# Landmark softmax in groups of two batches, two projection banks, zero matmuls in TensorE's waits, and half of the first attn1 exponentials inside the loop

## The chip, the cores and the metric

The kernel runs on one NeuronCore of a Trainium2 chip, as one program. The metric is the device time of one execution in microseconds (us); the time of a kernel is the median of its timed runs. Engines: PE is TensorE (PEld its weight load), DVE VectorE, ACT ScalarE, POOL GpSimd, SP SyncE. PS is PSUM, eight banks of 512 fp32 columns in 128 partitions.

## What is computed

Eight batches of small images and texts go through a tokenizer, a Nystrom attention layer (8 heads of 32), a mixture of experts, a second attention layer and a second mixture. The change touches the Nystrom attention. Cut to what matters:

```python
q_l = q.reshape(b, HEADS, LANDMARKS, l, DIM_HEAD).mean(3)
k_l = k.reshape(b, HEADS, LANDMARKS, l, DIM_HEAD).mean(3)
attn1 = softmax(einsum('bhid,bhjd->bhij', q, k_l), -1)
attn2 = softmax(einsum('bhid,bhjd->bhij', q_l, k_l), -1)
attn3 = softmax(einsum('bhid,bhjd->bhij', q_l, k), -1)
# _pinv(attn2): z0 scaled by the max of row and column sums over ALL batches and heads, then 6 steps:
az = a @ z
z = 0.25 * z @ (13.0 * I - az @ (15.0 * I - az @ (7.0 * I - az)))
out = attn1 @ attn2_inv @ (attn3 @ v) + conv(v)
```

The scale of the pseudo-inverse is a maximum over all batches. So attn2 of all eight batches must be ready before the first iteration of the first batch.

## The kernel before, in words

The block has a prologue and a loop over the eight batches (`body(b)`). Each engine has its own list of instructions, written out by hand in the order in which it runs them; semaphores (`wait_ge`, `then_inc`) tie the lists together. An engine that waits holds up everything behind it in its list.

Prologue, attn2. `proj(p, part)` (L740) projects the landmark tokens of a pair p of batches, part 0 for q and part 1 for k, into bank 4. ScalarE copies it out (`copied`, L919 and L921), and the next projection waits for that copy, since there is one bank. `scores(i)` (L752) makes the 8 heads' scores of batch i in banks 0 to 3. DVE takes the maximum (`shifted`, L1136) and subtracts it for half of the heads (L1141). ScalarE takes the exponential of four heads straight from PSUM, one instruction a head with its own bias and sum (`halved`, L930), and of the other four in one instruction (L934). `scores(i+1)` waits for both readers (`n_sub`, `n_half`). DVE sums and inverts (`summed`, L1149 to L1161), POOL multiplies (`normalised`, L985, signals `n_a`), TensorE adds row sums up (`sums`, L761). After the eighth batch DVE takes the maximum, TensorE spreads it (L791), DVE makes the scale `RCK` (signals `n_rck`), and ScalarE applies it in `opened` (L878).

Along with this the prologue does the front of batch 0: `project` (L561), `values` (L569), `scores3` (L583), `top3` (L1029) and `exps3` (L812) for attn3; `scores1` (L594), `top1` (L1040), `exps1` (L826) for attn1; `turn3` transposes (L601), `turned3`, `weigh` (L611), `turn_weighed` (L619), `small` (L1076), and `start` (L659).

Loop. A pass has 12 steps of TensorE (L677), k = 0 to 11, two per iteration of the inverse, each in two halves of four heads. An even step is read by DVE into NN (L1106); an odd one is added to TD and becomes ST (L1112). TD comes from POOL (L977), which needs SA, a scaling of ST on ScalarE (L895) that stands at the head of each iteration. Between the steps the table `FRONT` places the front of batch b+1, and `BACK` the end of batch b-1. In pass 0 alone `ffn_bias` (L636) and `value_out` (L644), both for later stages, and `turn1(0)` (L629) stand between the steps too. `start(b+1)` ends the pass.

Of the kernel before, what the change touches and what calls it, by code (L numbers as in the profile page):

```python
# [110 lines left out]
def program(nc, xpatch, txt, w1, ln1, vec, mat, wide, const, taps, out):  # L111
    with ExitStack() as ctx:
# [29 lines left out]
        WU = sb("WU", [1, 3])  # L142

# [18 lines left out]
        AA = fs("AA", [128, B, H, SW])  # L162

# [57 lines left out]
        with nc.Block() as block:  # L221
# [307 lines left out]
        SCORES, PROJ, PINV, TAIL = 0, 4, 4, 6  # L529
        SUMS, TOPS = 3, 1  # L530
# [17 lines left out]

        def quad(b, rows, width):

            return PS[0:rows, bank(b, 0):bank(b, 0) + 4, 0:width]

        with nc.Block() as block:
            @block.tensor
            def _(pe):

                def project(b):
                    if b:
                        pe.wait_ge(sem("f_pt"), upto(b - 1, 2, 2))
                    for j in range(4):  # L560
# [6 lines left out]
                def values(b):  # L567
                    for t in range(2):
                        last = nc.tensor.matmul(PS[0:UT, bank(b, 3), t * 256:(t + 1) * 256],  # L569
                                                XAP[:, b // 2, t * UT:(t + 1) * UT],  # L570
                                                MA[:, qkv(b) + 512:qkv(b) + 768], start=True, stop=True)
                    last.then_inc(sem("f_v"), 1)

                def scores3(b):
                    pe.wait_ge(sem("f_q"), upto(b, 1, 1))
# [22 lines left out]
                def turn3(b, t):  # L598
                    pe.wait_ge(sem("f_e1"), upto(b, 2, t + 1))
# [104 lines left out]
                def out_proj(b):  # L704

                    pe.wait_ge(sem("f_oo"), upto(b, 1, 1))
                    for hh in range(2):
# [5 lines left out]
                         9: weigh, 10: turn_weighed}  # L713
                BACK = {3: lambda b: attend(b, 0), 4: lambda b: attend(b, 1), 6: out_proj}

                def body(b):
                    for k in range(STEPS):
                        step(b, k // 2, k % 2)
                        if b == 0 and k == 0:
                            pe.wait_ge(sem("n_rck"), 1)  # L720
# [7 lines left out]
                        if b + 1 < B and k in FRONT:  # L728
                            FRONT[k](b + 1)
# [4 lines left out]
                def proj(p, part):  # L734
                    if 2 * p + part:
                        pe.wait_ge(sem("n_qk"), 2 * p + part)
                    for j in range(2):
                        for o in range(2):
                            w = qkv(o) + (2 * part + j) * 128
                            last = nc.tensor.matmul(PS[:, PROJ, (2 * j + o) * KP:(2 * j + o + 1) * KP], MA[:, w:w + 128],  # L740
# [3 lines left out]
                def scores(i):  # L744
                    pe.wait_ge(sem("n_qk"), 2 * (i // 2) + 2)
                    if i:
                        pe.wait_ge(sem("n_sub"), i)
                        pe.wait_ge(sem("n_half"), i)
                    for h in range(H):
                        r, hh = h % 4, h // 4  # L750
                        rows = slice(32 * r, 32 * r + 32)
                        last = nc.tensor.matmul(PS[0:KP, SCORES + r, hh * KP:(hh + 1) * KP], QL[rows, i // 2 % 3, hh, i % 2, :],  # L752
                                                QL[rows, i // 2 % 3, 2 + hh, i % 2, :], start=True, stop=True)
# [1519 lines left out]
```

## Time and profile before

| | us |
|---|---|
| median of 3 runs (728.40 to 735.58) | 730.26 |
| profiled execution | 736.04 |
| its span | 734.2 |
| PE busy | 681.5 (93%) |
| DVE, ACT, POOL busy | 413.5, 377.6, 229.7 |
| mean granted clock of TensorE | 0.939 |

Read it so: the profiled execution is some 6 us above the median of the runs, and sums are made against it. TensorE is busy for 93% of the span, but the share is a mean over stages. The page's row of the granted clock, in 40 slices of 18.4 us, shows where the clock was lower: `PEclk9997699999999999999958999957999999996999`. The fourth and fifth slices (55 to 92 us) are this block's prologue.

### The profile page before, as it was taken

How to read it: one execution, taken by the hardware profiler on the slowest of the kernel's cores; microseconds unless marked ns; L12 is line 12 of the kernel's file. 1: busy time of each engine (PE TensorE's matmuls, PEld its weight loads, DVE VectorE, ACT ScalarE, POOL GpSimd, SP SyncE). 2: the span in 40 equal slices, each digit the busy share in tenths (PEclk: the TensorE clock that was granted, in tenths of full speed). 3: DMA queues.
4: the chain of work that ended last, by engine and by line, in shares of the span. 5: the costliest groups of instructions: out<-in, count | busy, mean ns of one | idle time of the engine just before them, and what ended most of it. 6: DMA issues, size and time to landing. Idle time of an engine off the chain costs nothing. (4 is left out here: it accounts for less than half of the span.)

```text
span 734.2 us, 15178 instructions
## 1 busy us (share of the span) xinstructions
PE 681.5 (93%) x6033; PEld 527.5 (72%) x6033; DVE 413.5 (56%) x843; ACT 377.6 (51%) x1035; POOL 229.7 (31%) x204
## 2 busy tenths in 40 slices
PE   9887898999999999999889999869999999989896
PEld 5676798988989898988785555557666666647555
DVE  3457347667575767674525333426777777764322
ACT  4656447565655647473246555335555455544531
POOL 4155325343544344444300434023222222201001
PEclk9997699999999999999958999957999999996999
DMA  8200000000000000000000000000000000000000
GB/s 267 99 3 1 1 1 3 2 1 2 1 2 2 2 1 3 2 1 2 1 1 1 1 1 1 1 1 1 1 1 1 1 2 1 1 1 1 1 15 17
DMA packets 5214, 8.23 MB, mean 11 GB/s; under 512 B 3608, under 2 KB 4120, under 8 KB 4760
## 3 DMA queue, kind: packets, MB, share of 16 engines
q1 hardware_dynamic: 4552, 7.20, 3.1%
q8 instruction: 48, 0.79, 0.4%
q14 instruction: 22, 0.18, 0.1%
q10 hardware_dynamic: 592, 0.07, 0.1%
HBM read 6.71 MB, written 0.55 MB: 10 GB/s over the span
## 5 line engine op out<-in xcount | busy, mean ns | idle before, releaser
L977 POOL TENSOR_TENSOR STD<-STD,NN 91x492 f32<-91x492 f32 (+1 forms) x96 | 104.0, 1101 | 149.2 <-DVE NN L1106 78.7
L677 PE MATMUL PS<-ST 128*91 128x123 f32 x768 | 92.9, 272 | 4.8 <-DVE ST L1112 4.6
L1106 DVE SCALAR_TENSOR_TENSOR NN<-ST,PS 91x492 f32<-91x492 f32 x96 | 62.9, 661 | 56.3 <-PE PS L677 56.3
L677 PE MATMUL PS<-NN 128*91 128x123 f32 (+1 forms) x768 | 89.6, 268 | 3.2 <-DVE NN L1106 3.2
L677 PEld LDWEIGHTS PS<-ST 128*91 128x91 f32 x768 | 83.5, 159 | 11.0 <-DVE ST L1112 7.1
L677 PEld LDWEIGHTS PS<-NN 128*91 128x91 f32 x768 | 82.2, 160 | 10.4 <-DVE NN L1106 6.4
L1746 PE MATMUL PS<-QR,KA 128*128 128x270 f32 x256 | 72.2, 413 | 0.0
L895 ACT ACTIVATE STD<-ST 91x492 f32<-91x492 f32 (+1 forms) x96 | 51.6, 569 | 39.6 <-DVE ST L1112 39.6
L1860 DVE TENSOR_SCALAR CL<-PS,K 128x270 f32<-128x270 f32 x144 | 65.7, 496 | 9.8 <-PE PS L1746 4.5
L1112 DVE SCALAR_TENSOR_TENSOR ST<-PS,STD 91x492 f32<-91x492 f32 (+1 forms) x96 | 55.9, 599 | 22.1 <-POOL STD L977 12.4
L1801 ACT ACTIVATE EX<-CL,NG 128x540 f32<-128x540 f32 x64 | 46.7, 741 | 32.8 <-DVE CL L1860 32.7
L1508 ACT ACTIVATE GE<-PS,FB 128x540 f32<-128x540 f32 x64 | 42.4, 707 | 35.1 <-PE PS L1413 34.9
L1677 POOL TENSOR_TENSOR QR<-QR 64x540 f32<-64x540 f32 x32 | 34.6, 1082 | 68.4 <-ACT QR L1792 68.4
L1746 PEld LDWEIGHTS PS<-QR,KA 128*128 128x128 f32 x256 | 46.2, 194 | 10.8 <-issue 2.9
L826 ACT ACTIVATE E_<-PS,M 71x91 f32<-71x91 f32 x128 | 40.4, 344 | 9.8 <-DVE M L1040 9.8
L1413 PE MATMUL PS<-XM,MF 64*128 64x270 f32 x256 | 40.7, 440 | 0.1
L1837 DVE COPY KA<-PS 64x288 f32<-64x288 f32 x64 | 29.1, 454 | 20.3 <-PE PS L1687 17.9
L812 ACT ACTIVATE E<-PS,M 91x142 f32<-91x142 f32 x64 | 23.0, 372 | 28.5 <-DVE M L1029 28.5
L1761 PE MATMUL PS<-EX,VM 128*64 128x270 f32 x256 | 36.2, 404 | 0.0
L1433 PE MATMUL PS<-GE,WI 128*64 128x270 f32 x256 | 35.8, 403 | 0.0
L1413 PEld LDWEIGHTS PS<-XM,MF 64*128 64x128 f32 x256 | 23.1, 197 | 15.8 <-issue 8.2
L1792 ACT ACTIVATE QR<-PS 64x270 f32<-64x270 f32 x64 | 24.8, 388 | 18.5 <-PE PS L1687 18.1
(326 smaller groups left out, 1250.5 us busy)
## 6 DMA issues: line engine op xcount, KB each, us to landing
TP<-taps SPq DMA_DIRECT2D x1, 1204.0 KB, 16.1
MA<-mat SPq DMA_DIRECT2D x1, 1120.0 KB, 7.5
MF<-mat SPq DMA_DIRECT2D x1, 1024.0 KB, 12.6
WI<-wide SPq DMA_DIRECT2D x1, 902.0 KB, 9.0
CO<-const SPq DMA_DIRECT2D x1, 512.0 KB, 15.7
MQ<-mat SPq DMA_DIRECT2D x1, 512.0 KB, 16.4
out<-OS SPq DMA_DIRECT2D x8, 45.0 KB
XA<-xpatch SPq DMA_DIRECT2D x1, 256.0 KB, 2.8
```

The costliest lines, as they stand in the source:

```text
L677: last = nc.tensor.matmul(PS[0:NL, PINV + q, h % 4 * SW + c0:(h % 4 + 1) * SW], x[:, h, 0:NL], x[:, h, c0:SW], start=True, stop=True)
L826: last = nc.scalar.activation(E1_[:, h, t, :], PS[0:UT, bank(b, r), c:c + NL], ACT.Exp, bias=M1[:, hh, r, t:t + 1], accum_out=Z1[:, 0, 2 * ...
L895: nc.scalar.mul(SA[:, 4 * q:4 * q + 4, c0:SW], ST[0:NL, b % 2, 4 * q:4 * q + 4, c0:SW], S_D).then_inc(sem("f_sa"), 1)
L977: nc.gpsimd.tensor_tensor(TD[:, 4 * q:4 * q + 4, c0:SW], SA[:, 4 * q:4 * q + 4, c0:SW], NN[0:NL, 4 * q:4 * q + 4, c0:SW], ALU.subtract).th ...
L1106: v.scalar_tensor_tensor(out=NN[0:NL, own, :], in0=ST[0:NL, b % 2, own, :], scalar=N_S, in1=heads4(PS[0:NL, PINV + q, 0:4 * SW]), op0=ALU. ...
L1112: v.scalar_tensor_tensor(out=ST[0:NL, b % 2, own, c0:SW], in0=heads4(PS[0:NL, PINV + q, 0:4 * SW])[:, :, c0:SW], scalar=S_M, in1=TD[:, own ...
L1413: last = nc.tensor.matmul(PS[:, HIDDEN + 2 * (j % 2) + o, 0:NP], MF[half, j * 128:(j + 1) * 128], XM[half, p, :], start=True, stop=True)
L1508: nc.scalar.activation(GE[:, ring(p, j), :, :], PS[:, HIDDEN + 2 * (j % 2):HIDDEN + 2 * (j % 2) + 2, 0:NP], ACT.Gelu, bias=FB1[:, j:j + 1] ...
L1746: last = nc.tensor.matmul(PS[:, bank, 0:NP], KA[:, a, u, t * 128:(t + 1) * 128], QR[:, a, u, :], start=True, stop=True)
L1761: last = nc.tensor.matmul(PS[t * D:(t + 1) * D, 7 * o, 0:NP], VM[:, o, t, u * D:(u + 1) * D] if u < H else VR[:, o, t, :], EX[:, slot(i, o ...
L1801: nc.scalar.activation(EX[:, n, :, :], CL[:, n, :, :], ACT.Exp, scale=NG[:, u:u + 1]).then_inc(sem("d_e"), 1)
L1860: v.tensor_scalar(CL[:, slot(i, o, u), t, :], PS[:, bank, 0:NP], K2[:, a, c:c + 1], 0.0, ALU.add, ALU.max).then_inc(sem("d_cl"), 1)
```

## The change

Four edits, all in the prologue and the first pass.

1. The softmax of attn2 goes by pairs. `scores(p)` makes 16 matmuls, for both batches, in the same four banks (4 x 96 columns of each); `shifted`, `halved`, `other_half` and `summed` work on both, so each runs four times on twice the elements. `normalised` still works on one batch, two in a row.
2. `PROJ` becomes two banks, 4 for part 0 and 7 for part 1; a projection waits for the copy of its own bank. `values(0)` writes bank 5, and `scores1(0)` banks 0 to 3. The orders of TensorE, ScalarE and DVE in the prologue are written out anew; `small(0)` and `start(0)` move ahead of the scale. POOL does its five memsets at the start.
3. `spin(n, bank, low)`: n matmuls of zeros (256 columns, fp32, 32 output partitions that nothing reads), 1, 2, 2, 3 and 2 of them at five places of TensorE's list.
4. `exps1(0, 0)` stays in the prologue, behind `weighed(0)`; `exps1(0, 1)`, `total1`, `inverse1` and `normal1` of batch 0 go into iteration 0 of pass 0, and `turn1(0)` from step 0 to step 3. For this pass a table `FIRST` takes the place of `FRONT`, with the front of batch 1 one step later. Banks 1 to 3 still hold attn1's scores of batch 0, so `project(1)` waits for both halves of `exps1(0)`.

```diff
-        SCORES, PROJ, PINV, TAIL = 0, 4, 4, 6
-        SUMS, TOPS = 3, 1
+        SCORES, PROJ, PINV, TAIL = 0, (4, 7), 4, 6
+        SUMS, TOPS = 3, 4
...
                 def project(b):
-                    if b:
+                    if b > 1:
                         pe.wait_ge(sem("f_pt"), upto(b - 1, 2, 2))
+                    elif b:
+                        pe.wait_ge(sem("f_e1"), 2)
...
+                FIRST = {1: lambda b: (project(b), values(b)), 3: scores3, 6: scores1, 8: lambda b: turn3(b, 0), 9: lambda b: turn3(b, 1),
+                         10: weigh, 11: turn_weighed}
...
-                def scores(i):
-                    pe.wait_ge(sem("n_qk"), 2 * (i // 2) + 2)
-                    if i:
-                        pe.wait_ge(sem("n_sub"), i)
-                        pe.wait_ge(sem("n_half"), i)
+                def scores(p):
+                    pe.wait_ge(sem("n_qk"), 2 * p + 2)
+                    if p:
+                        pe.wait_ge(sem("n_sub"), p)
+                        pe.wait_ge(sem("n_half"), p)
...
+                FIRST = {1: query, 3: exps3, 7: lambda b: exps1(b, 0), 8: lambda b: exps1(b, 1), 9: turned3, 10: weighed}
...
-                def halved(i):
-
-                    act.wait_ge(sem("n_max"), i + 1)
-                    if i >= 2:
-                        act.wait_ge(sem("n_a"), i - 1)
-                    for h in (0, 1, 4, 5):
+                def halved(p):
+
+                    act.wait_ge(sem("n_max"), p + 1)
+                    if p >= 2:
+                        act.wait_ge(sem("n_a"), 2 * p - 2)
+                    for r in range(2):
+                        for g in range(4):
...
                 FRONT = {0: (key,), 1: (value,), 2: (top3,), 4: (total3,), 5: (top1, inverse3), 8: (total1, inverse1),
                          10: (small,)}
+                FIRST = {1: (key, value), 3: (top3,), 5: (total3,), 6: (top1, inverse3), 9: (total1, inverse1),
+                         11: (small,)}
```

TensorE's order in the last part of the prologue. Before, from the seventh scores (L752) on; L761 is `sums`, L601 `turn3`, L611 `weigh`, L791 the scale, L619 `turn_weighed`, L659 `start(0)`:

```order
L752 MATMUL PS<-STD 96x96 x8
L761 MATMUL PS<-AA,SL 32x91 x8
L752 MATMUL PS<-STD 96x96 x8
L761 MATMUL PS<-AA,SL 32x91 x8
L601 MATMUL PS<-CO,E 71x91 x16
L761 MATMUL PS<-AA,SL 32x91 x16
L611 MATMUL PS<-P,VU 32x91 x16
L791 MATMUL PS<-CG,ON 91x32
L619 MATMUL PS<-CO,WX 91x128 x2
L659 MATMUL PS<-AA 91x123 x8
```

Now, from the fourth and last scores (L778) on; L787 is `sums`, L169 the zeros, L611 `scores1(0)`, L621 `turn3`, L631 `weigh`, L639 `turn_weighed`, L679 `start(0)`, L828 the scale:

```order
L778 MATMUL PS<-STD 96x96 x16
L787 MATMUL PS<-AA,SL 32x91 x16
L169 MATMUL PS<-ZK 32x256 x3
L611 MATMUL PS<-KM,QM 71x91 x16
L621 MATMUL PS<-CO,E 71x91 x16
L787 MATMUL PS<-AA,SL 32x91 x16
L631 MATMUL PS<-P,VU 32x91 x16
L787 MATMUL PS<-AA,SL 32x91 x8
L639 MATMUL PS<-CO,WX 91x128 x2
L787 MATMUL PS<-AA,SL 32x91 x8
L679 MATMUL PS<-AA 91x123 x8
L828 MATMUL PS<-CG,ON 91x32
```

`scores1(0)` has come behind the last scores of attn2, and `start(0)` ahead of the scale.

TensorE's order in pass 0, steps 2 to 7 (a step is the row of eight matmuls 91x123). Before (L636 `ffn_bias`, L583 `scores3(1)`, L644 `value_out`, L594 `scores1(1)`, L677 a step):

```order
L677 MATMUL PS<-ST 91x123 x8
L636 MATMUL PS<-VE,MF 128x1 x16
L583 MATMUL PS<-KM,QM 91x142 x8
L677 MATMUL PS<-NN 91x123 x8
L644 MATMUL PS<-MV 64x64 x16
L677 MATMUL PS<-ST 91x123 x8
L677 MATMUL PS<-NN 91x123 x8
L594 MATMUL PS<-KM,QM 71x91 x16
L677 MATMUL PS<-ST 91x123 x8
```

Now (L656 `ffn_bias`, L649 `turn1(0)`, L664 `value_out`, L596 `scores3(1)`, L611 `scores1(1)`, L697 a step):

```order
L697 MATMUL PS<-ST 91x123 x8
L656 MATMUL PS<-VE,MF 128x1 x16
L697 MATMUL PS<-NN 91x123 x8
L649 MATMUL PS<-CO,P 91x71 x16
L664 MATMUL PS<-MV 64x64 x16
L596 MATMUL PS<-KM,QM 91x142 x8
L697 MATMUL PS<-ST 91x123 x8
L697 MATMUL PS<-NN 91x123 x8
L697 MATMUL PS<-ST 91x123 x8
L611 MATMUL PS<-KM,QM 71x91 x16
L697 MATMUL PS<-NN 91x123 x8
```

`scores3(1)` has moved from behind step 2 to behind step 3 and what follows it, and `scores1(1)` from behind step 5 to behind step 6.

ScalarE's order in pass 0, now (L933 the scaling into SA at the head of an iteration, two rows of it being the two halves; L848 `exps3(1)`, L863 `exps1(1)`, L905 and L902 parts for later stages):

```order
L848 ACTIVATE E,Z<-PS,M 91x142 x8
L933 ACTIVATE STD<-ST 91x492 x2
L905 ACTIVATE MF<-MF,VE 128x256
L902 ACTIVATE WH<-PS,VE 128x512
L933 ACTIVATE STD<-ST 91x492 x2
L905 ACTIVATE MF<-MF,VE 128x256
L863 ACTIVATE E_,Z<-PS,M 71x91 x8
L933 ACTIVATE STD<-ST 91x492 x2
L905 ACTIVATE MF<-MF,VE 128x256
L863 ACTIVATE E_,Z<-PS,M 71x91 x8
```

Before, both halves of `exps1(1)` stood ahead of the third of these scalings; now one stands on each side of it.

## Rows read from the trace of the kernel before

**Rows 1.** Table of stretches: busy us (instructions) by engine, granted clock, DMA.

```profile
core 0: us, PE busy (x) PEld busy (x) DVE busy (x) ACT busy (x) POOL busy (x), PEclk, DMA share, GB/s
36.40:53.50 17.10, 15.42 (x169) 13.62 (x169) 8.57 (x20) 9.12 (x37) 9.95 (x10) 1.00 0.01 2
...
56.90:67.20 10.30, 10.00 (x111) 9.07 (x110) 7.01 (x18) 7.34 (x41) 5.11 (x4) 0.50 0.01 2
...
74.00:84.50 10.50, 9.04 (x77) 7.81 (x77) 3.91 (x13) 4.03 (x16) 1.40 (x1) 0.50 0.01 2
...
87.70:101.30 13.60, 12.88 (x109) 12.04 (x108) 5.33 (x8) 5.28 (x10) 5.18 (x5) 1.00 0.00 1
101.30:126.70 25.40, 23.07 (x277) 21.08 (x277) 18.51 (x31) 17.82 (x69) 10.73 (x9) 0.93 0.01 2
126.70:160.90 34.20, 33.48 (x406) 30.46 (x404) 23.46 (x41) 20.16 (x72) 15.58 (x13) 1.00 0.01 2
```

**Rows 2.** Timeline, TensorE: start, us, shape, records (two a matmul), idle before.

```profile
36.43 1.10 PE L740 MATMUL PS<-XAP,MA 128*128 128x96 f32 x8 [1.09 <-PEq L127]
...
39.90 0.59 PE L752 MATMUL PS<-STD 32*96 32x96 f32 x16 [0.66 <-ACT STD L919]
...
45.59 1.03 PE L569 MATMUL PS<-MA,XAP 128*71 128x256 f32 x4
...
49.41 1.44 PE L761 MATMUL PS<-AA,SL 91*32 91x91 f32 x16
...
67.59 0.59 PE L752 MATMUL PS<-STD 32*96 32x96 f32 x16
...
76.03 2.64 PE L761 MATMUL PS<-AA,SL 91*32 91x91 f32 x16
...
84.49 3.45 PE L659 MATMUL PS<-AA 128*91 128x123 f32 x16 [0.51 <-DVE AA L1076]
87.77 2.05 PE L677 MATMUL PS<-ST 128*91 128x123 f32 x16
...
91.82 1.87 PE L561 MATMUL PS<-XAP,MA 128*128 128x238 f32 x8 [0.72 <-ACT PT L841]
...
97.87 3.87 PE L636 MATMUL PS<-VE,MF 64*128 64x1 f32 x32
...
106.69 1.93 PE L677 MATMUL PS<-ST 128*91 128x123 f32 x16
...
111.89 1.93 PE L677 MATMUL PS<-ST 128*91 128x123 f32 x16 [0.63 <-DVE ST L1112]
...
126.72 1.48 PE L659 MATMUL PS<-AA 128*91 128x123 f32 x12
```

**Rows 3.** Timeline, DVE and ScalarE behind the last scores of attn2.

```profile
69.31 0.90 DVE L1136 TENSOR_REDUCE MX<-PS 91x8 f32<-91x728 f32 x1
69.42 0.33 ACT L826 ACTIVATE E_<-PS,M 71x91 f32<-71x91 f32 x1 [1.57 <-DVE M L1040]
...
74.41 0.37 ACT L930 ACTIVATE EE<-PS,MX 91x91 f32<-91x91 f32 x1
...
75.66 0.56 ACT L934 ACTIVATE EE<-DD 91x364 f32<-91x364 f32 x1
```

**Rows 4.** Timeline, POOL's last normalisation and a DVE operation beside it.

```profile
77.55 1.40 POOL L985 TENSOR_TENSOR AA<-EE,ZR 91x728 f32<-91x728 f32 x1 [4.16 <-DVE ZR L1161]
77.61 1.36 DVE L1057 TENSOR_SCALAR Z<-Z,CO 91x8 f32<-91x8 f32 x1
```

**Rows 5.** Timeline, DVE's maximum and the first exponential of attn3.

```profile
58.14 1.33 DVE L1029 TENSOR_REDUCE M<-PS 91x8 f32<-91x1136 f32 x1
...
59.51 0.38 ACT L812 ACTIVATE E<-PS,M 91x142 f32<-91x142 f32 x1 [1.00 <-DVE M L1029]
```

**Rows 6.** Timeline, TensorE, zero matmuls of the stage before this block.

```profile
32.81 2.53 PE L352 MATMUL PS<-ZK 128*128 128x512 f32 x10
```

**Rows 7.** Timeline, POOL in pass 0, both halves of a subtraction.

```profile
97.94 2.40 POOL L977 TENSOR_TENSOR STD<-STD,NN 91x492 f32<-91x492 f32 x2 [5.91 <-DVE NN L1106]
```

More of the change, by code:

```diff
@@ L162, in program, with spin @@
         AA = fs("AA", [128, B, H, SW])
+        def spin(n, bank=7, low=0):
+            for _ in range(n):
+                if low:
+                    nc.tensor.matmul(PS[low:128, bank, 0:256], ZK[:, 0:128 - low].bitcast(F32), ZK[:, 0:256].bitcast(F32),
+                                     start=True, stop=True)
+                else:
+                    nc.tensor.matmul(PS[:, bank, :], ZK[:, 0:128], ZK[:, :], start=True, stop=True)
         def col(t, c, p=128, n=1):
@@ L806, in query, with exps3 @@
                                   ).then_inc(sem("f_q"), 1)
-                def exps3(b):
+                def exps3(b, first=0, end=H):
                     act.wait_ge(sem("f_m3"), upto(b, 1, 1))
-                    for h in range(H):
+                    for h in range(first, end):
                         r, hh = h % 4, h // 4
@@ L813, in exps3 @@
                                                     bias=M3[:, hh, r:r + 1], accum_out=Z3[:, 1, h:h + 1])
-                    last.then_inc(sem("f_e3"), 1)
+                    if end == H:
+                        last.then_inc(sem("f_e3"), 1)
                 def exps1(b, k):
@@ L899, in body @@
                         if b == 0 and it == 0:
-                            turned1(0)
+                            exps1(0, 1)
                         for k in (2 * it, 2 * it + 1):
@@ L938, in _ @@
-                ALONG = {0: query, 4: exps3, 6: both1, 7: turned3}
                 copied(0, 0)
                 copied(0, 1)
-                for i in range(B):
-                    if i + 1 < B // 2:
-                        copied(i + 1, 0)
-                    halved(i)
-                    if i == 7:
-                        act.wait_ge(sem("n_pad"), PADS)
-                    if i in ALONG:
-                        ALONG[i](0)
-                    if i + 1 < B // 2:
-                        copied(i + 1, 1)
+                copied(1, 0)
@@ new lines, in _ @@
+                copied(1, 1)
+                halved(0)
+                query(0)
+                copied(2, 0)
+                other_half(0)
+                copied(2, 1)
+                copied(3, 0)
+                halved(1)
+                other_half(1)
+                copied(3, 1)
+                halved(2)
+                other_half(2)
+                exps3(0, 0, 4)
+                halved(3)
+                other_half(3)
+                exps3(0, 4, H)
+                act.wait_ge(sem("n_pad"), PADS)
@@ L951, in _ @@
+                turned3(0)
                 weighed(0)
+                exps1(0, 0)
                 act.wait_ge(sem("n_rck"), 1)
@@ L1159, in summed @@
                     if i >= 2:
-                        dve.wait_ge(sem("n_a"), i - 1)
+                        dve.wait_ge(sem("n_a"), 2 * i - 2)
                     v.tensor_scalar(ZR[:, i % 2, :], z[:, 2, :], CO[0:NL, C_DV:C_DV + 1], None, ALU.mult
                                     ).then_inc(sem("n_zr"), 1)
-                ALONG = {0: (key,), 1: (value,), 3: (top3,), 5: (top1,), 6: (total3,)}
                 shifted(0)
-                for i in range(B):
-                    if i + 1 < B:
-                        shifted(i + 1)
-                    summed(i)
-                    for work in ALONG.get(i, ()):
-                        work(0)
+                key(0)
+                shifted(1)
+                value(0)
+                summed(0)
+                shifted(2)
+                top3(0)
+                summed(1)
+                shifted(3)
+                summed(2)
+                summed(3)
+                top1(0)
+                total3(0)
                 inverse3(0)
+                small(0)
                 sums = PS[KP:128, SUMS, 0:B * H // DH * NL].rearrange("p (g n) -> p g n", n=NL)
```

190 lines of the change are left out of this document (107 added, 83 removed).

## Prediction, made before the changed kernel ran

> **What bounds the kernel now.** I read the table of stretches first, for TensorE's busy time and granted clock [rows 1]. From 126.7 us on, one pass of the loop takes 34.2 us and TensorE is busy for 33.5 of them at full clock: the later passes are bound by TensorE, and the change leaves them alone. The stretches ahead of it are different: from 36.4 to 87.7 us (the landmark softmax) the clock is at its lower level for 56.9 to 67.2 and 74.0 to 87.7, and the first pass (87.7 to 126.7) has TensorE busy for 36.0 of 39.0 us. So I read TensorE's timeline next, which tells where each step stands [rows 2]. Two numbers come from there: 51.3 us from the first projection (36.43) to step 0 of the loop (87.77), and 39.0 us from step 0 to `start(1)` (126.72). Everything before 36.43 and behind 126.72 stays as it is.
>
> In the softmax, `scores(i)` starts at 39.90 for i=0 and at 67.59 for i=7: seven rounds of 3.96 us. One round is a ring: scores, DVE's max (0.91 us), ScalarE's four exponentials (74.41 to 75.66, so 0.31 us each with the read of the sum) and the next scores, which wait for `n_half` [rows 2, 3]. Behind the last scores there are 20.2 us to step 0: `top1(0)` stands ahead of DVE's last max (69.31), ScalarE then does all 16 exponentials of attn1 (69.42 to 74.41) before the last four of attn2, and the normalisation, `sums(7)`, the scale and `start(0)` follow, the latter two at the lower clock [rows 3, 4].
>
> **The change, part by part: eight rounds become four.** A round of two batches, from rows: 16 scores matmuls 0.9 us (two of the 0.59 us groups, tail off), max over 1456 elements 1.7 (0.91 us for 728 and 1.33 for 1136 give 1.03 ns an element), eight exponentials 2.5, hand-overs 0.2: 5.3 us [rows 2, 3, 5]. With two projection banks TensorE doesn't stop between the first projections, so scores(0) starts at 39.3 instead of 39.9. Round two also waits for two copies on ScalarE, whose projections stand behind `scores(1)` and `values(0)` (1.1 and 1.03 us): 6.9. Round three is 5.5. So scores(3) starts at 39.3+5.3+6.9+5.5 = 57.0, against 67.6.
>
> **The end of the prologue.** From scores(3) at 57.0: DVE has `top3(0)` and one `summed` ahead of the max, which ends at 60.1. Exponentials must wait for POOL's fourth normalisation (`n_a`; two of 1.40 us from 58.5) until 61.3; eight take 2.5, the other half 0.8 (0.56 for half the elements, part of it fixed), four of `exps3` 1.4 (0.38 each with overlap of the read): 66.1 [rows 3, 4, 5]. Transposes (0.8 and 0.8), then `turned3` (two of 0.8): 68.8. TensorE meanwhile adds `sums(4)` and `(5)`: 1.3 each at the full clock (1.44, its tail off), to 70.4; weigh 0.8, sums(6) 1.3, turn_weighed 0.4, sums(7) 1.3, `start(0)` 1.8: 76.0. The scale (0.5 on DVE) and `opened` (0.8) end at 77.7. Step 0 stands at 77.8 [rows 2, 3, 4]. The prologue is 41.4 us instead of 51.3: **minus 9.9**. All of it lies in fewer rounds; attn1's 16 exponentials leave the chain, eight of them into an idle ScalarE, eight into the loop.
>
> **The spins.** Ten matmuls of 256 columns. The nearest rows: 1.03 us for two of 256 columns in this number form, and 2.53 for ten of 512 in the fast form, so 0.25 to 0.5 each; by the nearer one 4.5 us in all [rows 2, 6]. They stand ahead of waits that are longer than they are (2.3, 2.9 and 2.4 us before scores(2), scores(3) and scores1), so I take 0.3 us on the path; uncovered they would cost all 4.5. Do zeros hold the clock? At 32.81 ten matmuls of ZK run and the clock stays at 1.00 behind them [rows 1, 6], so zeros work; those are of another form, full width, not 32 columns.
>
> **The first pass.** Three pieces. (a) Step 0 to step 4: 18.9 us before (87.77 to 106.69). The same TensorE work stands there after, tails off: four steps of 1.7, project 1.7, values 0.9, turn1 1.4, ffn_bias 3.8, value_out 1.1, scores3 0.6: 16.3, and 0.2 of hand-over [rows 2]. Now `project(1)` also waits until `exps1(0,1)` (2.5 us on ScalarE, behind two scalings) has read the banks: 1.0 us (before, it waited 0.72 for `turned1`). 17.5: minus 1.4. (b) Step 4 to step 6: 5.2 before (106.69 to 111.89), with scores1 inside. `scores3(1)` now comes one step later, and directly behind it `top3` (1.33), eight `exps3` (2.9) and the scalings for step 6 (0.6) follow one another, then POOL's subtraction 1.2 and DVE's 0.66: 7.1 from step 4, with TensorE holding only two steps (3.4) to hide it. Plus 1.9. (c) Step 6 to start(1): 14.8 before. Now scores1 0.9 falls in here; `top1` (1.8) stands ahead of the pass's ST, so step 8 starts 6.7 behind step 6; ScalarE's scalings stand between the two halves of `exps1(1)`, so the second transposes start at 12.3; step 10, weigh, step 11, turn_weighed and `small` give 18.1. Plus 3.3. Together **plus 3.7**: 42.7 instead of 39.0 [rows 2, 3, 5, 7].
>
> **The clock in the first pass.** ffn_bias (32 records of one column, 3.87 us) is followed by a stretch whose mean clock is 0.93 over 25.4 us, which at the two levels 1.2 and 2.4 GHz is some 3.5 us at the lower [rows 1, 2]. The same matmuls stand in the new pass, now ahead of step 3, turn1 and value_out, all TensorE-bound: 3.4 us at half clock lose 1.7, about 0.7 of which was paid before. **Plus 1.0.**
>
> **A cost that a page names.** DVE's TENSOR_SCALAR of 8 elements took 1.36 us while POOL normalised (77.55 to 78.95), and ended as POOL did [rows 4]. After, two normalisations stand back to back, and one such DVE operation can wait up to 1.4 us behind one. The one on the chain (`summed(3)`, 64.7 to 66.5) starts as POOL ends, so I take 0.1, bound 0 to 1.4. The Trainium skill, page "SBUF — State Buffer", section "Who interferes with whom", has it that DVE and GpSimd share one pair of ports under a lock held for a whole instruction. By that rule, the trace agrees.
>
> **Sum.** -9.9 + 0.3 + 3.7 + 1.0 + 0.1 = -4.8. The same durations and hand-overs, followed along the order of before, put start(1) at 127.8 where the trace has 126.72; I give half of that 1 us to the new chain too and take -5.3. The profiled execution took 736.0 us; the median of the three is 730.3. Predicted on the median: **725 us**.
>
> **Rivals.**
> *The gain stays whole* (chance 0.2): the stalls of (b) and (c) fill with waits that TensorE had anyway, the clock stays up: -9.9 + 1 = -9, 721 us. For it: before, TensorE also waited there (0.63 us before step 6) [rows 2]. Against: the exps3 and exps1 chains are in ScalarE's written order.
> *The clock falls in the prologue again* (0.2): the transposes and the waits around them are as they were ahead of 74.0, where it fell [rows 1]. Then four sums cost 1.2 more each (2.64 against 1.44), start(0) 1.4 more (3.45 against the 2.05 of a step with as many matmuls), less what waits hide: +5, and the sum is 0: 730 us. The Trainium skill, "TensorE: Matmul & The Clock Gate", "Part 4: PE-mode transpose", states that transposes don't count as a busy TensorE in the same way. By that rule, this rival is the case, and the spins around the transposes are what stands against it; the fall at 74.0 agrees with the rule.
> *Slower* (0.05): the waits of (b) (3.1 us of TensorE idle) pull the clock down and it stays down for the rest of the pass. Its 16 us of TensorE work then take up to 13 more; -5 + 13 = +8, 738 us. It decides once more than 5 us of added work at half clock come. Against: the work around those waits is of the same kind as in the later passes, which hold 1.00 [rows 1]; but no wait of 3 us stands in them.
>
> **How the numbers follow.** The forecast (prologue shorter, first pass longer) has 0.55; its own range is -2.5 to -7.5, that is 723 to 728. For 8 in 10 I add the whole gain below and the fallen clock above: 719 to 731. Faster by over 1% means under 723.0, slower means over 737.6 (1% is about what a measurement tells from no change): the whole-gain case and a sixth of the forecast and some of the spread of the runs (728.4 to 735.6) give 0.33; slower 0.05; within 1% 0.62.
>
> **What the changed profile would show.** Four rounds, scores starting near 39.3, 44.6, 51.5 and 57; step 0 near 78; project(1) behind exps1; a TensorE wait of about 3 us before step 6 and about 2 before step 8; start(1) near 121 (full clock) to 123; then passes of 34.2 us as before. Wrong would be: step 0 behind 82 (then the clock or POOL), or a first pass under 40 us (then (b) and (c)).

## The result, and the profile after

| | before | after |
|---|---|---|
| median of 20 runs, us | 732.04 (728.33 to 740.04) | 729.13 (726.22 to 731.82) |
| profiled execution, its span | 736.04, 734.2 | 729.43, 727.6 |
| mean granted clock | 0.939 | 0.952 |
| first projection to step 0 | 51.35 | 42.46 |
| step 0 to start(1) | 38.95 | 44.07 |
| start(1) to the end | 607.5 | 604.6 |

The ratio after to before is 0.9953, with a 95% interval of 0.9933 to 0.9972: the change saves 3.4 us (2.0 to 4.9); the two medians are 2.9 apart. The medians and ratios here and below leave out five slow executions: one of e3_exps_in_prologue (938 us), one of e4_ffn_bias_late (782 us) and three of `before` beside them (1072 to 1841 us). Forecast were 5.3 us less than 730.26, that is 725.0; measured are 729.13. The sign, the stages and nearly every wait came as forecast; the size did not. I use "start(1)" for the first of its matmuls (L679 now, L659 before), counted from the first projection, since everything ahead of the first projection is as it was.

First the page after, its first block and the row of the granted clock (40 slices of 18.2 us, tenths of full speed):

```profile
span 727.6 us, 15172 instructions
## 1 busy us (share of the span) xinstructions
PE 676.0 (93%) x6053; PEld 520.9 (72%) x6053; DVE 407.3 (56%) x815; ACT 377.0 (52%) x1031; POOL 229.5 (32%) x204
...
PEclk9998989999999999999969999958999999996999
```

Where `before` had `9997699` at its start, there is `9998989`: the softmax (fourth and fifth slice) has most of its clock back, and the first pass (fifth to seventh) has lost some. Next the stretches after, which answer to [rows 1] (busy us and instructions of each engine, then the granted clock):

```profile
core 0: us, PE busy (x) PEld busy (x) DVE busy (x) ACT busy (x) POOL busy (x), PEclk, DMA share, GB/s
36.40:53.60 17.20, 15.29 (x197) 13.09 (x198) 8.91 (x12) 10.64 (x43) 12.42 (x12) 1.00 0.01 1
53.60:60.40 6.80, 6.80 (x49) 5.49 (x49) 4.36 (x8) 4.75 (x25) 2.26 (x2) 0.50 0.01 4
60.40:78.90 18.50, 16.28 (x234) 13.73 (x227) 11.71 (x27) 9.97 (x47) 6.01 (x5) 1.00 0.01 2
78.90:97.60 18.70, 18.33 (x173) 17.12 (x173) 6.99 (x14) 7.93 (x27) 7.39 (x5) 0.91 0.00 1
97.60:104.70 7.10, 3.86 (x36) 3.44 (x32) 3.16 (x4) 4.97 (x21) 2.04 (x2) 1.00 0.00 0
104.70:123.00 18.30, 15.45 (x179) 14.16 (x179) 12.06 (x25) 12.38 (x48) 8.64 (x8) 0.91 0.01 2
123.00:157.20 34.20, 33.48 (x403) 30.45 (x403) 23.16 (x40) 20.18 (x72) 15.57 (x13) 1.00 0.01 2
```

The clock is at its lower level for 6.8 us of the softmax (before: 23.9, in two spells), and stays at 1.00 through the end of the prologue, where before it had fallen at 74.0. The first pass is rows four to six: step 0 to 4, step 4 to 6, step 6 to start(1). In the fifth TensorE is busy for 3.9 of 7.1 us. The second pass takes 34.2 us, as before. And TensorE's timeline after, which answers to [rows 2] (start, us, shape, records, idle before and its releaser):

```profile
36.44 2.89 PE L765 MATMUL PS<-XAP,MA 128*128 128x96 f32 x24 [1.09 <-PEq L127]
39.26 0.93 PE L778 MATMUL PS<-STD 32*96 32x96 f32 x32
...
44.74 0.93 PE L778 MATMUL PS<-STD 32*96 32x96 f32 x32 [0.43 <-ACT EE L972]
...
51.62 0.93 PE L778 MATMUL PS<-STD 32*96 32x96 f32 x32 [1.31 <-ACT EE L972]
...
53.35 4.82 PE L787 MATMUL PS<-AA,SL 91*32 91x91 f32 x32
57.97 1.91 PE L169 MATMUL PS<-ZK 128*32 128x256 f32 x4
59.81 1.23 PE L778 MATMUL PS<-STD 32*96 32x96 f32 x32
...
67.62 1.47 PE L621 MATMUL PS<-CO,E 91*71 91x91 f32 x16 [1.18 <-ACT E L848]
...
78.90 1.94 PE L697 MATMUL PS<-ST 128*91 128x123 f32 x16 [0.42 <-ACT ST L917]
...
83.05 1.87 PE L570 MATMUL PS<-XAP,MA 128*128 128x238 f32 x8 [0.37 <-ACT E_ L863]
...
87.41 3.73 PE L656 MATMUL PS<-VE,MF 64*128 64x1 f32 x32
...
97.60 1.93 PE L697 MATMUL PS<-ST 128*91 128x123 f32 x16
...
104.70 3.48 PE L697 MATMUL PS<-ST 128*91 128x123 f32 x16 [3.07 <-DVE ST L1166]
...
111.83 1.93 PE L697 MATMUL PS<-ST 128*91 128x123 f32 x16 [0.95 <-DVE ST L1166]
...
117.47 0.85 PE L621 MATMUL PS<-CO,E 91*71 91x91 f32 x8 [1.39 <-ACT E_ L863]
...
122.97 1.93 PE L679 MATMUL PS<-AA 128*91 128x123 f32 x16 [0.51 <-DVE AA L1128]
```

Four rounds of scores (L778) stand at 39.26, 44.74, 51.62 and 59.81. The first three are where they were forecast; the fourth is 2.8 us late, since two sums took 4.82 us at the lower clock (53.35; 2.70 in the next pair) and the two matmuls of zeros behind them 1.91 instead of 1.03, with no wait left for them to lie in. Step 0 is at 78.90, step 4 at 97.60, step 6 at 104.70 behind the new wait of 3.07 us, start(1) at 122.97.

### The profile page after: what moved, and what is told of

The parts are those of the page before. It is cut to its first block and busy times, and to the rows that moved or that the text cites. A ratio compares the mean times of both kernels' runs of the same rounds, so it can differ in the third digit from the quotient of the medians.

```text
span 727.6 us, 15172 instructions
## 1 busy us (share of the span) xinstructions
PE 676.0 (93%) x6053; PEld 520.9 (72%) x6053; DVE 407.3 (56%) x815; ACT 377.0 (52%) x1031; POOL 229.5 (32%) x204
## 5 line engine op out<-in xcount | busy, mean ns | idle before, releaser
L697 PE MATMUL PS<-ST 128*91 128x123 f32 x768 | 94.1, 274 | 8.5 <-DVE ST L1166 8.0
L697 PEld LDWEIGHTS PS<-ST 128*91 128x91 f32 x768 | 84.9, 161 | 14.9 <-DVE ST L1166 10.4
L697 PE MATMUL PS<-NN 128*91 128x123 f32 (+1 forms) x768 | 90.3, 269 | 2.2 <-DVE NN L1160 2.1
L697 PEld LDWEIGHTS PS<-NN 128*91 128x91 f32 x768 | 82.5, 161 | 9.1 <-DVE NN L1160 5.4
L933 ACT ACTIVATE STD<-ST 91x492 f32<-91x492 f32 (+1 forms) x96 | 51.6, 571 | 37.2 <-DVE ST L1166 37.2
L863 ACT ACTIVATE E_<-PS,M 71x91 f32<-71x91 f32 x128 | 40.5, 345 | 11.2 <-DVE M L1092 11.2
L848 ACT ACTIVATE E<-PS,M 91x142 f32<-91x142 f32 x64 | 23.0, 376 | 22.4 <-DVE M L1081 22.4
L1850 ACT ACTIVATE QR<-PS 64x270 f32<-64x270 f32 x64 | 24.8, 388 | 18.6 <-PE PS L1745 18.2
```

What stands on the lines that cost most here:

```text
L697: last = nc.tensor.matmul(PS[0:NL, PINV + q, h % 4 * SW + c0:(h % 4 + 1) * SW], x[:, h, 0:NL], x[:, h, c0:SW], start=True, stop=True)
L863: last = nc.scalar.activation(E1_[:, h, t, :], PS[0:UT, r, c:c + NL], ACT.Exp, bias=M1[:, hh, r, t:t + 1], accum_out=Z1[:, 0, 2 * h + t:2 ...
L933: nc.scalar.mul(SA[:, 4 * q:4 * q + 4, c0:SW], ST[0:NL, b % 2, 4 * q:4 * q + 4, c0:SW], S_D).then_inc(sem("f_sa"), 1)
```

## The experiments

One execution is a thin base here, as the first experiment shows. The table has the markers of every profile, all counted from that kernel's first projection (35.94 to 38.60 us), and the microseconds at the lower clock in the softmax, in pass 0 and behind start(1) ("rest"). Each row is one execution.

| kernel | step 0 | pass 0 | start(1) | rest | low clock, softmax / pass 0 / rest |
|---|---|---|---|---|---|
| before | 51.35 | 38.95 | 90.29 | 607.5 | 23.9 / 3.4 / 62.9 |
| e5_before_again | 49.87 | 38.93 | 88.80 | 601.9 | 20.5 / 3.4 / 49.7 |
| e6_before_third | 49.87 | 38.93 | 88.80 | 601.9 | 20.5 / 3.4 / 49.6 |
| after | 42.46 | 44.07 | 86.53 | 604.6 | 6.8 / 6.8 / 56.1 |
| e7_after_again | 40.66 | 44.07 | 84.73 | 602.0 | 0 / 6.8 / 49.7 |
| e11_after_timed | 40.92 | 46.23 | 87.15 | 604.7 | 3.4 / 13.7 / 56.0 |
| e1_no_zeros | 44.67 | 42.32 | 86.99 | 607.7 | 10.2 / 3.4 / 62.9 |
| e2_zeros_alone | 53.01 | 38.89 | 91.90 | 602.0 | 10.2 / 3.4 / 49.5 |
| e9_one_bank | 43.35 | 46.16 | 89.50 | 601.8 | 3.4 / 13.7 / 49.6 |
| e3_exps_in_prologue | 40.92 | 42.79 | 83.71 | 601.9 | 3.4 / 10.2 / 49.7 |
| e4_ffn_bias_late | 40.64 | 41.36 | 82.00 | 606.0 | 0 / 6.8 / 59.7 |
| e8_front_and_late_bias | 42.45 | 41.14 | 83.59 | 607.6 | 6.8 / 10.2 / 62.9 |
| e10_more_zeros | 42.69 | 39.47 | 82.16 | 601.8 | 6.8 / 6.8 / 49.7 |

**The same programs again: e5_before_again, e6_before_third, e7_after_again, e11_after_timed.** No edit. The question was whether the two profiled executions stood for their programs.

> The kernel before, unchanged, for a second profile. Its first had the clock low for 10.2 and 13.7 us in the landmark softmax, with step 0 51.35 us and start(1) 90.29 us behind the first projection. Theory A (the forecast was sized against an execution that was slower than most, which is where 2 us of the expected gain went): low for less than 20 us here, start(1) at 87.5 to 89.5 us. Theory B (that profile was typical): start(1) at 90 to 91 us.

> The kernel before, unchanged, for a third profile, with the same two theories: A, start(1) at 87.5 to 89.5 us behind the first projection and less than 20 us at the lower clock in the landmark softmax; B, 90 to 91 us as in the first profile.

> The changed kernel, unchanged, for a second profile. In its first the clock was low for 6.8 us in the softmax and for 3.4 us twice in pass 0; step 0 stood 42.46 us and start(1) 86.53 us behind the first projection. Theory A (the clock's spells lie differently from execution to execution): step 0 at 40.6 to 43 and start(1) at 84.5 to 87.5, with other spells. Theory B (the spells belong to the order of work): the same spells within 1 us, start(1) within 0.5 us of 86.53.

> The changed kernel, unchanged, timed beside the two others of this call. Both theories of its shortfall: ratio 0.993 to 0.997; a third profile. Theory A (spells lie by chance): start(1) at 84.7 to 87 us behind the first projection, by the number of microseconds at the lower clock. Theory B: 86.53 again.

Measured: `before` took 730.88 and 730.13 us, `after` 724.85; timed once more in e11_after_timed, `after` had 729.60 and the ratio 0.9957 (0.9927 to 0.9987), the same as the first time. The execution of `before` on which my sum stood, 736.04, was 5 to 6 us above these two of the same program. The table says where: 1.5 us in the softmax, where the clock was low for 23.9 us instead of 20.5, and 5.6 us behind start(1), with 62.9 us at the lower clock instead of 49.7. Against that, its first projection came 1.2 to 1.9 us sooner (36.43; 37.67 and 38.36 in the other two, which had 3.4 us of low clock ahead of it). Over the three profiles of each kernel the means are 50.36 and 41.35 to step 0 (-9.0), 38.94 and 44.79 for pass 0 (+5.9), 89.30 and 86.14 to start(1) (-3.2), and 603.8 and 603.8 behind it. -3.2 agrees with the timed -3.4: the effect lies ahead of start(1), and behind it the two programs don't differ by more than one program does from itself. Three profiles of each are few: start(1) spreads over 1.5 us in `before` and 2.4 in `after`, so these means are no surer than about 1 us. The two spells of pass 0 in `after` came again in e7_after_again, at the same places. Within `after` pass 0 varies with the clock too. Two stretches of e11_after_timed:

```profile
89.00:102.70 13.70, 13.70 (x104) 13.11 (x105) 3.42 (x5) 2.52 (x9) 2.00 (x2) 0.50 0.00 0
102.70:124.00 21.30, 16.39 (x198) 14.69 (x197) 13.52 (x27) 16.09 (x62) 10.71 (x9) 1.00 0.01 2
```

The clock fell 2.7 us into ffn_bias (86.37 to 90.95) and came back only behind 13.7 us, in all of which TensorE was busy. Step 0 to 4 then took 22.1 us instead of 18.7, yet the pass only 2.2 more than in `after`, because `after` had its second spell in the last part, which e11 ran at full clock.

**e1_no_zeros.** `after` without its ten matmuls of zeros.

```diff
-                spin(1, SCORES, 96)
                 scores(1)
...
-                spin(2, SCORES, 96)
                 scores(2)
...
-                spin(2, SCORES, 96)
                 scores(3)
...
-                spin(3, SCORES, 96)
                 scores1(0)
...
-                spin(2, TOPS, 96)
```

> The changed kernel without its ten zero matmuls in the landmark softmax and ahead of step 0. In its own trace the clock falls at 53.65 us for 6.8 us although the zeros are there. Theory A (the zeros buy little here): the clock is low for 7 to 14 us of the prologue instead of 6.8, step 0 stands at 78 to 80 us (78.90 with them), ratio to the kernel before 0.995 to 0.998. Theory B (the zeros carry the gain): low clock as before, for 20 us or more, step 0 behind 82, ratio 0.999 to 1.002.

Measured 732.99 us, ratio 1.0002 (0.9975 to 1.003). By the timed runs nothing is left of the gain without the zeros: they are worth some 3.5 us, with a wide margin, since this interval and that of `after` (0.9933 to 0.9972) all but touch. The ratio is that of theory B, the low clock (10.2 us) that of theory A. TensorE's timeline of e1:

```profile
45.20 0.93 PE L778 MATMUL PS<-STD 32*96 32x96 f32 x32 [0.98 <-ACT EE L972]
...
52.09 0.93 PE L778 MATMUL PS<-STD 32*96 32x96 f32 x32 [2.29 <-ACT EE L972]
...
57.56 0.93 PE L778 MATMUL PS<-STD 32*96 32x96 f32 x32 [1.04 <-ACT EE L972]
...
64.23 1.29 PE L611 MATMUL PS<-KM,QM 32*71 32x91 f32 x32 [1.37 <-ACT EE L972]
66.27 2.70 PE L621 MATMUL PS<-CO,E 91*71 91x91 f32 x16 [0.75 <-ACT E L848]
68.90 4.61 PE L787 MATMUL PS<-AA,SL 91*32 91x91 f32 x29
...
98.64 1.93 PE L697 MATMUL PS<-ST 128*91 128x123 f32 x16
...
105.74 3.44 PE L697 MATMUL PS<-ST 128*91 128x123 f32 x16 [3.07 <-DVE ST L1166]
...
123.90 1.93 PE L679 MATMUL PS<-AA 128*91 128x123 f32 x16 [0.51 <-DVE AA L1128]
```

Counted from the first projection (36.91), the second to fourth scores stand at 8.29, 15.18 and 20.65 us. In e11_after_timed, with zeros, they stand at 8.30, 15.19 and 20.66. So at full clock the zeros cost nothing on the path; the waits of 0.98, 2.29 and 1.04 us are what they fill (0.44, 1.31 and 0.18 are left). What they do is further on: here the clock fell to 0.50 at 64.5 for 10.2 us, behind a wait of 1.37 us ahead of scores1, and ran the transposes and four sums in 2.70 and 4.61 us for 29 records instead of 1.47 and 2.46. Step 0 comes at +44.67 instead of +40.7 or +40.9. This is my second rival, priced at +5 us, and it measures +4 in the prologue. In none of the eight profiles of this order with zeros did the clock fall between scores1 and step 0; that the three zero matmuls ahead of scores1 are what keeps it up rests on this one profile without them.

Where the timed 3.5 us lie this profile does not show. Its start(1) stands at +86.99, between the +84.73 and +87.15 of `after`, because its pass 0 had one spell less (42.32 us); its stretch behind start(1) is long, 607.7 us, but `before` and e8 have one of 607.5 and 607.6 too.

And zeros are not free once the clock is low. In `after` the two ahead of the last scores end at 59.81, and TensorE goes from the sums straight through them; in e7_after_again, at full clock, they leave a wait:

```profile
55.82 1.03 PE L169 MATMUL PS<-ZK 128*32 128x256 f32 x4
57.02 0.93 PE L778 MATMUL PS<-STD 32*96 32x96 f32 x32 [0.18 <-ACT EE L972]
```

Without them the last scores of `after` could have started at 57.97 instead of 59.81. By that estimate the zeros cost 1.8 us there, about what its step 0 is behind that of e7_after_again (+42.46 against +40.66).

**e2_zeros_alone.** `before` with 14 such matmuls: one ahead of each scores from the second on, 3 and 2 ahead of the halves of `turn3(0)`, 2 ahead of the last sums; their tile stays in memory for them.

```diff
+                def idle(n):
+                    for _ in range(n):
+                        nc.tensor.matmul(PS[96:128, SCORES, 0:256], ZK[:, 0:32].bitcast(F32), ZK[:, 0:256].bitcast(F32),
+                                         start=True, stop=True)
```

> The kernel before, in its own order of eight rounds, with 14 such zero matmuls: one ahead of each scores(i) from i=1, three and two ahead of the two groups of transposes, two ahead of the last sums. It tells what a held clock is worth without the other edits. Theory A (the rounds carry the gain, the clock is worth a part): the clock is low for less than the 24 us of before, step 0 at 84 to 87.5 us (87.77 before), ratio 0.996 to 1.000. Theory B (the clock carries the gain): step 0 at 80 to 83, ratio 0.990 to 0.995.

Measured 731.0 us, ratio 0.9986 (0.9961 to 1.0011): no change that can be told. The low clock in the softmax went from 20.5 to 10.2 us, but 6.8 us of it fell early, at 40.3, over projections, 7.8 us before the first of the added zeros (48.16). TensorE's timeline of e2:

```profile
41.27 0.97 PE L752 MATMUL PS<-STD 32*96 32x96 f32 x16 [0.66 <-ACT STD L929]
42.17 2.02 PE L740 MATMUL PS<-XAP,MA 128*128 128x96 f32 x8
43.98 3.38 PE L561 MATMUL PS<-XAP,MA 128*128 128x238 f32 x8
...
48.16 0.62 PE L774 MATMUL PS<-ZK 128*32 128x256 f32 x2
48.70 0.59 PE L752 MATMUL PS<-STD 32*96 32x96 f32 x16
```

The second scores are 7.43 us behind the first instead of 4.08 (e5_before_again), because TensorE has no wait there in the old order: 2.02 and 3.38 us instead of 1.13 and 1.80 at the lower clock, and the zeros' 0.62 us on top. Step 0 comes at +53.01 instead of +49.87, and I had expected it at 84 to 87.5 us where it stands at 90.74. Most of that is the early spell, which came before any of the added matmuls. Behind it one can compare: from the second to the eighth scores e2 takes 25.0 us and e5_before_again 23.6, from there to step 0 17.0 and 18.7. So the rounds, which have little wait for the zeros, take 1.4 us more, although less of them is at the lower clock, and the part behind them, now at full clock, 1.7 less: nothing in sum, as timed.

**e9_one_bank.** `after` with both parts of a projection in bank 4.

```diff
-        SCORES, PROJ, PINV, TAIL = 0, (4, 7), 4, 6
+        SCORES, PROJ, PINV, TAIL = 0, (4, 4), 4, 6
...
-                    if p:
-                        pe.wait_ge(sem("n_qk"), 2 * (p - 1) + part + 1)
+                    if 2 * p + part:
+                        pe.wait_ge(sem("n_qk"), 2 * p + part)
```

> The changed kernel with the projections in one bank again (bank 4; each waits for the copy before it), all else as changed. Theory A (the second bank is a small part, the pairs are the gain): scores(0) later by 1.5 us than with two banks (4.3 instead of 2.8 us behind the first projection), step 0 at 42.5 to 45 us (40.66 and 42.46 with two), ratio 0.996 to 0.999. Theory B (the bank is idle cover, its wait hides): step 0 within 0.5 us of the two-bank kernel at the same clock, ratio 0.994 to 0.996.

Measured 730.55 us, ratio 0.998 (0.9952 to 1.0008), beside 0.9957 for `after` on the same chip. The timed gap is 1 to 2 us and the intervals overlap. The timelines tell it better, since both had 3.4 us of low clock in the softmax: first scores at +4.44 instead of +2.82, step 0 at +43.35 instead of +40.92. In these two profiles the second bank is worth 2.4 us. It takes away four waits for a copy of 0.57 or 0.58 us and what follows from them:

```profile
37.62 1.13 PE L765 MATMUL PS<-XAP,MA 128*128 128x96 f32 x8 [0.58 <-ACT STD L962]
39.32 1.13 PE L765 MATMUL PS<-XAP,MA 128*128 128x96 f32 x8 [0.57 <-ACT STD L960]
...
49.23 1.13 PE L765 MATMUL PS<-XAP,MA 128*128 128x96 f32 x8 [0.57 <-ACT STD L960]
50.95 1.13 PE L765 MATMUL PS<-XAP,MA 128*128 128x96 f32 x8 [0.58 <-ACT STD L962]
```

**e3_exps_in_prologue.** The fourth edit undone: all 16 exponentials, sums and the normalisation of attn1(0) back in the prologue, `turn1(0)` at step 0, `project(1)` no longer behind `exps1(0)`, and the old table for pass 0.

```diff
-                        if b == 0 and k == 3:
+                        if b == 0 and k == 0:
...
-                        front = FRONT if b else FIRST
+                        front = FRONT
...
-                            exps1(0, 1)
+                            turned1(0)
...
-                exps1(0, 0)
+                both1 = (exps1(0, 0), exps1(0, 1))
```

> The changed kernel with its fourth edit undone: both halves of exps1(0) behind weighed(0), total1, inverse1 and normal1 ahead of the loop, turn1(0) behind step 0, and the front of batch 1 placed in pass 0 as in all the others (FRONT, no FIRST). Theory A (the late front of batch 1 is what makes pass 0 44.1 us long instead of 39.0): ScalarE waits 2.7 us for the scale anyway and takes the eight exponentials there, so step 0 stays within 1 us of 78.9; no 3 us wait before step 6; start(1) at 118 to 120 us instead of 122.97, ratio 0.988 to 0.991. Theory B (the exponentials were rightly moved): step 0 is late by their 2.5 us, pass 0 gains no more than that, start(1) within 1 us of 122.97, ratio 0.994 to 0.997.

Measured 726.84 us, ratio 0.9926 (0.9897 to 0.9956), beside 0.9953 and 0.9957 for `after`: undoing the fourth edit gains about 2 us by the medians, less than theory A had it, and the intervals overlap. The profile points the same way: start(1) at +83.71, against +84.73 to +87.15. Step 0 is at +40.92, no later than in `after`. ScalarE shows why; first e7_after_again, then e3, ahead of the scale (L916):

```profile
73.12 0.22 ACT L863 ACTIVATION_READ_ACCUMULATOR E_<-PS,M 71x1 f32 x1
76.25 0.56 ACT L916 ACTIVATE ST<-PS,RCK 91x364 f32<-91x364 f32 x1 [2.91 <-DVE RCK L1249]
```

```profile
76.52 0.25 ACT L863 ACTIVATION_READ_ACCUMULATOR E_<-PS,M 71x1 f32 x1
77.17 0.56 ACT L916 ACTIVATE ST<-PS,RCK 91x364 f32<-91x364 f32 x1 [0.40 <-DVE RCK L1249]
```

ScalarE has 2.91 us with nothing to do ahead of the scale, and the eight exponentials that the change carried into the loop fill 2.5 of them. With `FRONT` the wait of 3.07 us in pass 0 is gone too; its place is taken by the 0.63 us of [rows 2]:

```profile
105.89 1.93 PE L697 MATMUL PS<-ST 128*91 128x123 f32 x16 [0.63 <-DVE ST L1166]
```

**e4_ffn_bias_late.** `ffn_bias` from behind step 2 to behind step 5, ahead of that wait, with DVE's read of it and ScalarE's first preparation.

```diff
-                        if b == 0 and k == 2:
+                        if b == 0 and k == 5:
...
-                PREPARED = {1: (8,), 3: (9,), 4: (0, 10), 7: (1,), 8: (2,), 9: (3, 4), 10: (5,), 11: (6, 7)}
+                PREPARED = {1: (8,), 3: (9,), 4: (10,), 7: (0, 1), 8: (2,), 9: (3, 4), 10: (5,), 11: (6, 7)}
...
-                            if b == 0 and k == 3:
+                            if b == 0 and k == 6:
```

> The changed kernel with ffn_bias behind step 5 instead of step 2 (and its two readers moved to match), into TensorE's wait of 3.07 us ahead of step 6. Theory A (that wait is a chain on ScalarE, POOL and DVE that TensorE can fill): start(1) at 120 to 121 us instead of 122.97, ratio 0.991 to 0.993. Theory B (the chain to step 6 starts behind TensorE's work and moves only in part, or the clock that falls behind the one-column matmuls eats it): start(1) at 122 or later, ratio 0.994 or more.

Measured 724.92 us, ratio 0.9897 (0.9854 to 0.9939, from five executions), and pass 0 in 41.36 us instead of 44.07 at the same 6.8 us of low clock:

```profile
95.63 4.32 PE L656 MATMUL PS<-VE,MF 64*128 64x1 f32 x32
99.88 3.59 PE L697 MATMUL PS<-ST 128*91 128x123 f32 x16
```

ffn_bias takes the place of the 3.07 us; step 6 follows it with no wait. So the wait in (b), step 4 to step 6, was real idle time of TensorE, and 2.7 us of the longer pass come from the order, not from what has to be done.

**e8_front_and_late_bias.** e3 and the idea of e4 together; with the old table the waits are at steps 6 and 7, so ffn_bias goes behind step 6.

```diff
-                        if b == 0 and k == 2:
+                        if b == 0 and k == 6:
```

> The changed kernel with both halves of exps1(0) in the prologue, the usual table for pass 0, and ffn_bias behind step 6, where TensorE waited 1.23 us ahead of step 7. If the gains of the two runs before add up in part (pass 0 of 42.8 us with the exponentials in the prologue, 41.4 with the bias late): start(1) at 80 to 81.5 us behind the first projection against 83.71 and 82.00, ratio to the kernel before 0.985 to 0.989. If they are the same microseconds: start(1) at 82 to 83.7, ratio 0.989 to 0.993.

Measured 721.5 us, ratio 0.9855 (0.9823 to 0.9888): 1.5% faster than `before`, and 1.0% faster than `after`. The ratio is what I had expected if the two gains add up; the profile is not, with start(1) at +83.59 instead of +80 to +81.5. That execution was the slowest of the seven (728.99, the others 720.68 to 722.46), with 17 us of low clock ahead of start(1) and 62.9 behind it. Pass 0 settles it at equal low clock: with 6.8 us of it, it takes 44.07 us in `after`, 41.36 in e4 and 39.47 in e10_more_zeros, which has this order; with 10.2 us, 42.79 in e3 and 41.14 here. So the gains add up in good part. Against e4 alone the intervals overlap.

**e10_more_zeros.** e8 with six matmuls of zeros ahead of the third scores instead of two, to keep the clock up at the sums behind it.

```diff
-                spin(2, SCORES, 96)
+                spin(6, SCORES, 96)
                 scores(2)
```

> The kernel of e8 with six zero matmuls instead of two ahead of scores(2), where TensorE waited 1.31 us and behind which the clock fell in two of four profiles (17.2 us behind the first projection). Theory A (the fall comes from that wait): no low clock in the softmax, step 0 at 40.7 to 41.5, ratio 0.982 to 0.987. Theory B (the fall is elsewhere, or 1.7 us of zeros delay scores(2) by more than they save): ratio 0.986 to 0.990.

Measured 724.53 us, ratio 0.9899 (0.9869 to 0.9929), against 0.9855 for e8 on another chip: no gain, if anything a loss, as theory B had it. The last scores come 0.35 us later than in e11_after_timed (21.01 us behind the first projection against 20.66). The clock didn't fall at 17.2 us behind the first projection this time, but at 23.3, for 6.8 us, over the sums behind the last scores. More zeros there didn't keep the clock up through the softmax.

## Why the prediction was right in its steps and wrong in its size

**Rounds: right.** Scores were forecast at 39.3, 44.6, 51.5 and 57.0. In e7_after_again (first projection at 36.36), which had no low clock in the softmax, they stand at 39.18, 44.66, 51.55 and 57.02. Step 0 was forecast at 77.8, and stands at 77.02 there, at 77.86 in e11 and at 78.90 in `after`. But that all of the gain "lies in fewer rounds" the runs don't bear out: without zeros (e1) step 0 is at +44.67, so up to 4 of the 9 us depend on the clock that stays up.

**The base of minus 9.9: wrong, and the first step that failed.** The softmax of `before` was taken as 51.3 us from one execution. Two more have 49.87. With the 0.3 of the zeros and the 0.1 of the port I had -9.5; the means of three and three give -9.0. The new chain came 0.4 us sooner than my sum (41.35 against 41.8), the old one was 1.0 us shorter than I took it (in the mean of three). I had seen that the profiled execution was 6 us above the median and yet read each stage as if all of it were the program's.

**Zeros: right that they lie in waits, wrong in one part.** Their cost is 0.0 us at full clock, not 0.3, and by estimate 1.8 in `after`, where the clock fell ahead of them. The clock held at the transposes with them and not without them (e1), but even with them it fell at the sums behind the third scores (`after`) or the fourth (e11).

**Pass 0: +4.7 forecast, +5.9 measured, and two errors in it.** Pieces (a), (b) and (c) without a spell can be read one by one, from two executions. In e1, (a) is 81.58 to 98.64: 17.1 us (forecast 17.5; `project(1)` waits 0.37, not 1.0). (b) is 7.1 (forecast 7.1), with a wait of 3.07 (3.1). (c) at full clock is in e11, 107.03 to 124.09: 17.1 (forecast 18.1; the wait before step 8 is 0.95 in `after`, not 2). That makes 41.2 where I had 42.7: the order costs 2.3 us, not 3.7. **The term of the clock is the one that was mis-sized most:** +1.0 forecast, +3.6 measured (the mean of 44.79 less 41.2). The two errors partly cancel, which is luck. In `after` one spell of 3.4 us behind ffn_bias made (a) 18.7 (+1.6), as forecast in kind, and a second one behind the new wait of 3.07 us made (c) 18.3 (+1.2): +2.8. In e11 one spell of 13.7 us behind ffn_bias made +5.0. I had given the wait no price in the forecast, only in the rival "slower". That rival's condition does occur: the clock fell for 3.4 us within 0.6 us of the start of step 6 in the three profiles in which TensorE had waited 3.07 or 3.08 us for it (`after`, e7, e1), and not in e11 and e9, where the wait was 2.00 and 1.94. Whether it is the wait that does it no run isolates. It costs 1.2 us and not 13, because the clock came back after 3.4 us.

**"I take -5.3": wrong.** Half of 1 us was added for a difference between my chain and the trace of `before`. No row stood behind it, and nothing in the runs bears it out. Together: 0.5 (softmax) + 1.2 (pass 0) + 0.5 make 2.2 us, and 5.3 less the 3.2 of the profiles is 2.1. Each of these pieces is no surer than about 1 us, as said above. In the absolute number 1.8 us more comes from the median of three runs, 730.26, where twenty have 732.04.

**The port.** The row of `before` [rows 4] has its like after. DVE's operation of 16 elements at 67.12 takes 0.18 us everywhere else in this softmax, and here 1.06, until POOL ends at 68.15:

```profile
65.39 2.76 POOL L1041 TENSOR_TENSOR AA<-EE,ZR 91x728 f32<-91x728 f32 x2 [4.49 <-DVE ZR L1216]
```

```profile
67.12 1.06 DVE L1208 SCALAR_TENSOR_TENSOR ZZ<-EE,ZZ 91x16 f32<-91x16 f32 x1
```

In e7_after_again the same operation took 0.18: there POOL had ended. So the operation is held up for 0 to 0.9 us, within the bound of 0 to 1.4. It cost nothing on the path: from the transposes to step 0 both executions take 11.28 us (67.62 to 78.90, 65.74 to 77.02). The trace agrees with the rule of the Trainium skill, "SBUF — State Buffer", "Who interferes with whom".

**The rivals.** "The gain stays whole" is out: both waits are there. "The clock falls in the prologue again" did not happen at the transposes: in the three profiles of `after` they run at full clock (1.47 us for 16 records), and without zeros (e1) the clock fell at 64.5, behind a wait and ahead of the transposes at 66.27. In e5_before_again it fell at 71.8 for the second time, also ahead of the first transposes (74.05), and in e6_before_third at 71.2 (73.34); only in the first profile of `before` did it fall behind them (74.0 and 72.09). By the Trainium skill, "TensorE: Matmul & The Clock Gate", "Part 4: PE-mode transpose", transposes don't count as a busy TensorE in the same way, and by that rule this rival would have been the case; these traces speak against it as the cause here.

**What stays open.** Why the clock falls at the sums in one execution of `after` and not in the next, and why e2's fell at 40.3, where no other profile has it low. And where the 3.5 us lie that the runs without zeros take longer.

## What to carry to other kernels

Take two or three profiles of the kernel before and compare them stage by stage before summing: a term of 9 us was off by 1 because it was read against one execution. Where an engine waits at a new place, look first for late-needed work that can stand there (ffn_bias: 2.7 us of pass 0), and before carrying work off an engine, look at its idle time at that spot: the eight exponentials fitted into 2.91 us of nothing. Matmuls of zeros inside a wait cost nothing measurable here at full clock, and the runs without them were some 3.5 us longer; where the wait was gone, because the clock was low, they stood on the path themselves.

## What the runs showed of the hardware that I had not expected

The same program on the same data loses its clock at different places from one execution to the next: 49.5 to 62.9 us at the lower level behind start(1), which alone moves that stretch from 601.8 to 607.7 us, 0.4 us for each microsecond at the lower level. Much of the spread of the runs goes with the clock: of the twenty of `after`, the three with a mean granted clock of 0.959 took 726.2 to 726.6 us, and the two with 0.945 took 731.8. And 32 records of one column each (ffn_bias, 3.7 to 4.8 us in which the profile has TensorE busy) had a low clock at their end or within 1.5 us behind them in twelve of the thirteen profiles (e1 is the one without): 3.4 us of it in seven of them, 6.8 to 13.7 in the other five.
